# Row maxima of an attention kernel spread by DMA instead of by TensorE, in a pipeline two slots deeper

## The reference, cut to what matters

```python
x = x + tanh(g_xattn) * attention(layernorm(x), ctx)   # 32 heads of 128, 8 key/value heads
x = x + tanh(g_ffn) * ffn(layernorm(x))                # 512x512 base, 8 low-rank experts, best 2
# attention, per batch (4), 256 queries, 1601 keys, float32:
scores = einsum('bkglm', q, k) / sqrt(128)
attn = softmax(scores)          # exp(scores - rowmax) / rowsum
o = einsum(attn, v); return o @ Wo + bo
```

## Time and profile before

| | before |
|---|---|
| median of 3 runs | 2283.16 us (2281.47 to 2284.03) |
| the profiled execution | 2283.97 us |
| its span, first to last instruction | 2281.9 us |
| PE busy | 98% |
| DVE, ACT, POOL busy | 80%, 75%, 71% |
| granted TensorE clock | 0.999 |

### The profile page before, as it was taken

One profiled execution on the slowest core, in us unless ns is written; L12 is line 12 of the kernel. 1 busy time (PEld: TensorE's weight loads), 2 busy tenths in 40 slices (PEclk: granted clock), 3 DMA queues, 4 the chain that ended last, 5 costly groups with the idle time before them and its releaser, 6 DMA issues.

```text
span 2281.9 us, 37476 instructions
## 1 busy us (share of the span) xinstructions
PE 2239.7 (98%) x12299; PEld 1930.6 (85%) x12299; DVE 1814.5 (80%) x3199; ACT 1712.2 (75%) x3248; POOL 1624.6 (71%) x1373
## 2 busy tenths in 40 slices
PE   6999999999999999999999999999999999999999
PEld 6888888888888888888888888888888888888875
DVE  5888888888787787787878787787787878787786
ACT  4777777777777777777777777777777777777773
POOL 5987887967668678767757778667757657667672
PEclk9999999999999999999999999999999999999999
DMA  7444343455233342426214343333423213222221
GB/s 262 142 151 138 120 165 122 159 192 173 90 115 111 103 159 94 136 82 212 93 49 135 118 132 113 113 133 112 169 85 103 93 63 102 75 91 91 77 91 37
DMA packets 140031, 273.97 MB, mean 120 GB/s; under 512 B 22048, under 2 KB 57408, under 8 KB 139584
## 3 DMA queue, kind: packets, MB, share of 16 engines
q1 hardware_dynamic: 124864, 257.85, 33.5%
q10 hardware_dynamic: 14976, 13.74, 2.9%
HBM read 202.44 MB, written 66.97 MB: 118 GB/s over the span
## 4 chain that ended last, share of the span: by engine, by line
PE 75%; DVE 11%; POOL 5%; issue 4%; ACT 4%; DMA 1%; ACTq 0%; SPq 0%; POOLq 0%; DVEq 0%
PE psW L456 11%; PE psW L458 11%; PE psW L457 11%; PE psS L456 6%; PE psS L458 6%; PE psS L457 6%; PE psW L686 6%; PE psW L689 5%; PE psW L688 5%; DVE psum_ L1444 3%; DVE mrun L1411 3%; POOL xs L900 2%; PE psW L513 2%; DVE pl L1164 2%; PE psW L521 1%
## 5 line engine op out<-in xcount | busy, mean ns | idle before, releaser
L900 POOL TENSOR_TENSOR xs<-xs,mb 128x512 f32<-128x512 f32 x832 | 1062.3, 1301 | 452.7 <-ACT mb L971 452.7
L1411 DVE TENSOR_TENSOR mrun<-psS,mrun 128x512 f32<-128x512 f32 (+1 forms) x704 | 482.4, 685 | 276.5 <-ACT xs L971 273.2
L971 ACT ACTIVATE xs<-psS 128x512 f32<-128x512 f32 x832 | 497.9, 599 | 216.9 <-PE psS L458 205.6
L1164 DVE TENSOR_TENSOR pl<-psP,ph 128x512 fp32r<-128x512 f32 (+1 forms) x672 | 459.6, 684 | 127.5 <-ACT ph L1106 126.6
L1106 ACT ACTIVATE ph<-xs 128x512 fp32r<-128x512 f32 x832 | 521.0, 626 | 2.8 <-PE psW L689 0.9
L1444 DVE TENSOR_TENSOR psum_<-psP,psum_ 128x512 f32<-128x512 f32 (+1 forms) x672 | 457.5, 681 | 0.0
L1101 ACT ACTIVATE psP<-xs 128x512 f32<-128x512 f32 (+1 forms) x672 | 402.5, 599 | 32.2 <-POOL xs L900 13.7
L456 PE MATMUL psS<-ql,kh 128*128 128x512 f32 x832 | 341.6, 411 | 7.8 <-DVE mrun L1411 6.6
L686 PE MATMUL psW<-ph,vh 128*128 128x512 f32 x832 | 336.1, 404 | 2.8 <-POOL pl L904 1.1
L457 PE MATMUL psS<-qh,kh 128*128 128x512 f32 x832 | 327.4, 393 | 0.0
L458 PE MATMUL psS<-qh,kl 128*128 128x512 f32 x832 | 326.8, 393 | 0.0
(11 more groups left out here) (225 smaller groups left out, 4436.4 us busy)
## 6 DMA issues: line engine op xcount, KB each, us to landing
wqh<-scr_wq SPq DMA_DIRECT2D x96, 256.0 KB, 2.6
wql<-scr_wq SPq DMA_DIRECT2D x96, 256.0 KB, 2.9
woh<-scr_wo SPq DMA_DIRECT2D x47, 512.0 KB, 3.3
wol<-scr_wo SPq DMA_DIRECT2D x47, 512.0 KB, 4.2
rbc<-scr_r ACTq DMA_DIRECT2D x52, 256.0 KB, 3.6
scr_wq<-wqh SPq DMA_DIRECT2D x32, 256.0 KB, 2.4
scr_wq<-wql SPq DMA_DIRECT2D x32, 256.0 KB, 3.1
scr_wo<-woh SPq DMA_DIRECT2D x16, 512.0 KB, 2.6
```

Of the source, the lines that this page charges most:

```text
L900: eng.tensor_tensor(tile, tile, mb[:, U % 2, :], ALU.subtract).then_inc(s_sub)
L971: return eng.activation(hi, src, ACT.Copy)
L1164: return eng.tensor_tensor(lo, src, f32(hi), ALU.subtract)
L1411: eng.tensor_tensor(run, psS[0:rows, s % 2, :], a, ALU.max).then_inc(s_m)
```

## The change

For units 2 to 62 job b, ScalarE's copy of mb and the waits that go with them are taken out. Instead ScalarE issues two DMAs: in slot 2 of the next unit, `max_to_memory` writes nm (128x4) to a scratch in memory; in slot 3, `max_to_lanes` reads it back to all lanes, straight into mb. GpSimd waits for that DMA. Subtraction, exponential and PV of a tile come two slots later (SUB, EXP, VAL 16, 17, 19 become 18, 19, 21), the ring xs has 20 tiles instead of 19. The division goes from slots 9 and 10 to 11 and 12 (10 and 11 where the sum goes by PE), the sum's DMAs from slots 6 and 7 to 8 and 9, s from slot 5 to 6 or 7. The output projection moves wholly into the third unit after (p0, p1), two halves in each unit of four, where before the four units had 2, 0, 3 and 3. The special tables LAST_BUT_ONE and TURN are gone. In the drain the last layer's jobs are spread over two more slots.

```diff
-    SUB, EXP, VAL = 16, 17, 19
-    RX, RP = 19, 3
+    SUB, EXP, VAL = 18, 19, 21
+    RX, RP = 20, 3
...
+    def max_by_mem(U):
+        return MEM_LO <= U < UN - 1
...
-        return 9 if sum_by_mem(V) else 8 if V < UN - 2 else 10 if V == UN - 2 else 6
+        return NT * (V + 2) + (ON if sum_by_mem(V) else 10 if V < UN - 2 else 12 if V == UN - 2 else 8)
+    SW = 8
+    SR = 9
+    MW = 2
+    MR = 3
+    ON = 11
...
     AT_MEM = [
-        "m q0 b k3 q1 s v0 v1 v2 v3 v4 o0 o1",
-        "m,v5 v6 b q0 k0 s,v7 v8 k1 q1 v9 - v10 -",
-        "m,v11 - b,v12 k2 p0 s k3 r,p1 q0 - q1 x0 o0,x1",
-        "m q0 b k0 p1 s k1 - q1 k2 - o0 o1",
+        "p0,m - p1 - q0 k3 q1 s v0 v1 v2 v3 v4",
+        "v5,q0,m - v6 p0 p1 v7 k0 s,v8 - q1 k1 v9 v10",
+        "m - v11 k2 v12 p0,p1 k3,s q0 - q1,r - - x0,x1",
+        "p0,m - p1 - q0 k0 - k1,s - q1 - k2 -",
     ]
...
-                if kind == "r" and sum_by_mem(n):
+                if kind == "r" and sum_by_mem(n) or kind == "b" and max_by_mem(n):
                     continue
...
+            def max_to_memory(n):
+                i = maxes_by_mem(n) - 1
+                act.wait_ge(s_nm, n + 1)
+                if i >= 2:
+                    act.wait_ge(s_md, 16 * (i - 1))
+                eng.dma_start(scr_m[i % 2], nm[:, n % 2, :]).then_inc(s_mw, 16)
+
+            def max_to_lanes(n):
+                act.wait_ge(s_mw, 16 * maxes_by_mem(n))
+                act.wait_ge(s_sub, NT * (n - 1))
+                eng.dma_start(mb[:, n % 2, :], scr_m[(maxes_by_mem(n) - 1) % 2].rearrange("p k -> (p k)").partition_broadcast(128)).then_inc(s_md, 16)
...
+                if w == MW and max_by_mem(W + 1):
+                    max_to_memory(W + 1)
+                if w == MR and max_by_mem(W + 1):
+                    max_to_lanes(W + 1)
```

More of the change, by code:

```diff
@@ L79, in sums_by_mem, with maxes_by_pe, maxes_by_mem @@
         return U + 1 - sums_by_pe(U)
[L81 to L83 removed]
+    def max_by_mem(U):
+        return MEM_LO <= U < UN - 1
+    def maxes_by_pe(U):
+        return sum(not max_by_mem(u) for u in range(U + 1))
+    def maxes_by_mem(U):
+        return U + 1 - maxes_by_pe(U)
+    def on_slot(V):
+        return NT * (V + 2) + (ON if sum_by_mem(V) else 10 if V < UN - 2 else 12 if V == UN - 2 else 8)
[4 more added lines that the diff above has]
+    ON = 11
     jobs = {s: [] for s in range(SLOTS)}
     AT = [
[4 rows of a table removed]
[4 rows of a table added]
     ]
     AT_MEM = [
[4 rows of a table removed]
[L98 to L102 removed]
[4 rows of a table added]
+    ]
     for U in range(UN + 2):
[L105 to L107 removed]
+        names_of = {0: "k1 - k2 v0 q0 k3 q1 v1 - v2 - v3 -", UN: "p0 - p1 - - - - - - - s r -",
+                    UN + 1: "- p0 - p1 c - s - o0 o1",
+                    UN - 1: "m p0 - - p1 - - s - r - - -"}.get(U, (AT_MEM if U >= MEM_LO + 2 else AT)[U % 4])
         for t, names in enumerate(names_of.split()):
@@ L624, in job @@
                     pe.wait_ge(s_nm, n + 1)
-                    spread(("b", n, 0), nm[:, n % 2, :], s_bt, s_mb, n + 1)
+                    spread(("b", n, 0), nm[:, n % 2, :], s_bt, s_mb, maxes_by_pe(n))
                 elif kind == "r":
@@ L693, in _ @@
                         eng.matmul(o, vb[0:n, hs], pl[0:n, T % RP, :], start=False, stop=True).then_inc(s_pv)
-                if s // NT >= 2 and s % NT == on_slot(s // NT - 2) + 2:
-                    emptied(("pv", s // NT - 2, 0), s_ol, s // NT - 1)
+                for V in range(UN):
+                    if s == on_slot(V) + 2:
+                        emptied(("pv", V, 0), s_ol, V + 1)
                 if s == TN + 7:
@@ L1069, in _ @@
             for s in range(SLOTS):
-                V = s // NT - 2
+                V = next((V for V in range(UN) if s == on_slot(V)), -1)
                 if s < TN:
@@ L1132, in _ @@
                         ffn_inner(n)
-                if 0 <= V < UN and s % NT == on_slot(V) and not sum_by_mem(V):
+                if V >= 0 and not sum_by_mem(V):
                     divided(V)
@@ L1331, in after_job @@
                     lower_x(n, part)
-                elif kind == "o" and n < UN - 1 and (n, part) != (UN - 3, 0):
+                elif kind == "o" and n < UN - 1:
                     add_o(n, part)
@@ L1415, in _ @@
                 b, u = divmod(U, NU)
-                V = U - 2
+                V = next((V for V in range(UN) if 0 <= s - on_slot(V) <= 1), -1)
                 for j in jobs.get(s - 1, []):
@@ L1419, in _ @@
                         after_job(*j)
-                if sum_by_mem(V):
-                    divide(V, t - on_slot(V))
+                if V >= 0 and sum_by_mem(V):
+                    divide(V, s - on_slot(V))
                 if s < TN - 1:
@@ L1425, in _ @@
                     running_max(TN - 1)
-                    add_o(UN - 3, 0)
                     row_max(UN - 1)
-                if 0 <= V < UN and not sum_by_mem(V):
-                    divide(V, t - on_slot(V))
+                if V >= 0 and not sum_by_mem(V):
+                    divide(V, s - on_slot(V))
                 for j in jobs.get(s - 1, []):
```

47 lines of the change are left out of this document (27 added, 20 removed), and 8 rows, old and new, of the table AT.

## The result

The changed kernel took 2350.38 us (median; 2346.11 to 2353.85) against 2283.17 (2281.47 to 2284.03) before: the ratio is 1.0294, 95% interval 1.0276 to 1.0313. The prediction was 2275, range 2258 to 2291. The kernel became slower, on the side to which 0.19 was given, and by far more than its slower rival (2295).

The account below looks back on a forecast made before the run. TensorE was busy 98%, but VectorE's 1.8 us against 1.39 was taken to bound bare slots. Terms -21.4 - 18.8 - 7.8 - 2 + 1 + 40.6 = -8.4 from 2283.97 gave 2275 us as a median, range 2258 to 2291.

Parts of the forecast that it names:

- the path of mb by DMA: Maxima written and read back in slots 2 and 3; mb lands 9 us after slot 1 begins, margin 1.6: zero cost.
- the chain at the ends of units: New TensorE waits from third to fourth and fourth to first units, behind the division: +40.6 us in all.
- the old waits: Waits in third units (18.8 us) and the extra time of units 4 to 15 (7.8 us) go: 26.6 us.
- b, 0.35 us in 61 units: The four small matmuls that spread the maxima, taken from units 2 to 62: 21.4 us off TensorE.
- The chain from the multiplication on: End of third units: from the multiplication, low part of slot 11 at +2.49 us and ol at +3.70.
- The walk: Timing from S(10) in third units, TensorE arriving undelayed: multiplication at 3.93 us, 2.8 us wait where the sum goes by memory.
- rival (b): Slower: mb lands late in units with SyncE's loads, 2.0 us in a third of 30 units; 2295 us, chance 0.17.
- GpSimd's splits of Wo at zero: Slots 6 and 7 of a unit, needed in the next unit, GpSimd idle 29%: no cost.
- ScalarE's waits for the maxima's pair: Slots 2 and 3: waits for nm and for the write cost ScalarE about 1 us, which it can spare.
- The tail, +1: Two more slots at the back, beside TensorE's work for the last layer: +1 us, bounds -1 and +4.
- The start, -2: Fewer waits in units 1 to 3: -2 us, bounds -4 and +2.

Follow-up runs that it names:

- the run with SyncE: The changed kernel with the write and read of the reciprocal sums issued by SyncE at the start of slot 8, not by ScalarE: 2329.69 us.
- two tries: Against the kernel with load, splits, oh and SyncE edits (2281.10 us): third units' p0, p1 in slots 8, 10, 2298.60; another order in two units of sixteen, 2308.58.

## Why the prediction was wrong, by its own steps

The prediction missed the profiled difference by 77.5 us (-8.4 against +69.1). The step that failed most is the path of mb by DMA, put at nothing with a margin of 1.6 us and measured at 33.6. Then come the chain at the ends of units (40.6 against 60.2) and the old waits (26.6 expected to go, some 14.5 went). The clock had no term: it was read at 2.4 GHz in every slice of the kernel before and kept for a kernel with longer waits. Its 12 us at most lie in these terms.

- **b, 0.35 us in 61 units: right.** The two kernels that differ by it alone are 18.9 us apart.
- **The chain from the multiplication on: right** to 0.02 us, and with it the places of the new waits (third to fourth, fourth to first unit) and what ends them. Its size was not: 60 us measured for 40.6. The walk let the multiplication start 3.93 after S(10); it was 5.06. The step that failed is the sum's write, which I had seen (it "has a bare slot before it") and left to the bounds. That explains 1.1 us of the 1.4 by which a third unit by memory was short; an earlier write gave back 0.6 of it, and 1.4 with the time lost at the lower clock taken out.
- **"Old waits that go", 26.6: wrong**, about 14 by what is left in the table, which no run isolates. I read the 0.63 us before S(12) in the earlier trace rows as belonging to slots that the table fills, and so did away with it. It belongs to the order on ScalarE and VectorE, oh ahead of the exponentials (0.41 us idle ahead of oh in the same rows), which the change keeps: moving oh takes 17 us from the kernel before and 28 from the changed one. The term was also too large: it took unit 22 for all 15 third units, but slot 11 of units 18, 34 and 50, whose sum goes by PE, took 1.50 us in the kernel before and not 2.18.
- **The DMA path at zero, margin 1.6 us: wrong**, 34 us in the profile of 2350 us (some 22 in those of 2338), the splits of the next point and the clock behind these waits included; the load alone is 7 to 12. From unit 16 on mb came at 11.5 to 11.6 in first and fourth units instead of 9, since the read took 6.1 to 6.3 and not 3.6. This is rival (b)'s mechanism, with its place right. Its price per unit (a us of PE for each us past 10.6) held about: 11.6 means 1, and slots 8 and 9 lost 0.3 to 2.0 from unit 16 on. What failed is how many: a third of 30 units at 2 us; it was nearly all, and those of the first batch too, where there is no such load and the write lands late instead (2.9 us in the median of first units). The Trainium skill (Trainium Kernel Development and Optimization, Key Constraints) says that DMAs from these queues interleave on the same engines; the reads of 6.1 to 6.3 us with such a load beside 3.9 to 4.2 without agree.
- **GpSimd's splits of Wo at zero** ("GpSimd is idle 29%"): wrong, 2 to 6 us. The idle share said nothing of the stretch between mb and its first low part, in which GpSimd has no time at all: in unit 8 a half's two operations, 1.9 us, stand there, and TensorE waits 1.80 us behind them.
- **ScalarE's waits for the maxima's pair, about 1 us a unit: right in size**, 35.1 us for nm and 7.7 for the write in 61 units. What cost time is the same wait of the sum's pair, which had no term of its own: 8.4 us by the run with SyncE.
- **The tail, +1: wrong**, +6.2. I took the two slots at the back as 0.69 each. From the last slot of scores to the end of the drain 22 groups of probability matmuls now take 43.9 us; before, 20 took 38.4, so two more cost 5.5. The first and the last of the 22:

```profile
2276.49 0.39 PE L701 MATMUL psW<-ph,vh 128*128 128x512 f32 x1
...
2320.42 0.80 PE L701 MATMUL psW<-ph,vh 128*128 128x512 f32 x1
```

- **The start, -2: right** (-2.9).
- **The range** left out half of (b) and had no case in which (b) and a longer walk come together. Both hang on DMAs that ScalarE issues in order, and should not have been weighed as if only one could be true.

What stays open: what ends the last 1.6 to 2.2 us at third units (two tries moved them), what makes the clock fall behind some waits and not behind others, and the 12 us between the changed kernel's two times (its clock is much the same in both).

## What to carry to other kernels

Behind a wait in an in-order queue stands all that comes later in it. A DMA pair on a compute engine costs not its issue (0.33 us) but the wait for the write, at its worst landing and not its median; a queue that has slack, here SyncE's, is the place for it. Before filling idle slots of the bounding engine, look whether two others wait for each other in program order: one instruction moved was worth 17 and 28 us here, while four new orders of jobs won 2 us at most and lost up to 31. And a slack that is an average over the span (GpSimd's 29%) is not a slack in the one stretch that counts. When an edit gains more or less than its waits explain, compare the granted clock of the two runs first: a wait of TensorE can cost once more behind it.

## What the runs showed of the hardware

- A write of 2 KB landed in 1.4 us at best, and in 7.25 at worst while SyncE moved weights; the median of the earlier trace rows, 1.8, says little of it.
- A read of 256 KB to all lanes took 3.3 to 4.1 us from unit 16 on with the output weights' load three slots later, and up to 7.8 beside it.
- The same code took 2350 us in one set of runs and 2338 in two others, with medians of 4.4 and 3.8 us for the read of mb, while the kernel before stayed at 2282 to 2283. That the spread of the DMAs makes the difference is likely, but not shown.
- TensorE's granted clock fell to 1.2 GHz right behind waits of 0.9 to 2.9 us and not behind all of them; matmuls of 512 columns then start 0.42 us apart instead of 0.23. The mean clock ran from 0.988 to 1.000 over these kernels, some 28 us to none (estimate).
